# A linear-attention layer with an FP4 gate on one NeuronCore: gate and up in parts of 384 and 320 channels, two groups of tensors moved by 128 bytes

## The reference, cut to what matters

```python
q, k, v = (xn @ W + b for W, b in (Wq, bq), (Wk, bk), (Wv, bv))    # 16 heads of 64
Q, K = elu(q) + 1, elu(k) + 1
KV = einsum('bshd,bshm->bhdm', K, v)
Z = 1 / (einsum('bshd,bhd->bsh', Q, K.sum(axis=1)) + 1e-6)
o = einsum('bshd,bhdm,bsh->bshm', Q, KV, Z)
x = layer_norm(xn + o @ Wo + bo)
s = layer_norm(x + gelu(x @ W1 + b1) @ W2 + b2)
# the other branch; fq quantizes blocks of 16 along the last axis to FP4 and back
gate, up = fq(xn) @ fq(w_gate).T, fq(xn) @ fq(w_up).T              # 704 channels each
h = silu(gate) * up
g = silu(fq(h) @ fq(w_down).T)
out = src + s * g
```

## Time and profile before

| | |
|---|---|
| median of 3 runs | 1651.9 us (1649.95 to 1652.05) |
| the profiled execution, its own time | 1650.24 us |
| its span, first to last instruction | 1648.5 us |
| mean granted TensorE clock | 0.997 of full |
| TensorE (PE) busy | 1608.9 us, 98% |
| weight loads (PEld) busy | 1444.7 us, 88% |
| VectorE (DVE) busy | 1278.5 us, 78% |
| ScalarE (ACT) busy | 979.4 us, 59% |
| GpSimd (POOL) busy | 782.8 us, 47% |
| DMA, mean | 75 GB/s |

### The profile page before, as it was taken

The page is one execution under the profiler, slowest core; times in us unless marked ns, Lnnn a source line. Parts: engine busy times, 40 slices in busy tenths (PEclk is TensorE's granted clock), DMA queues, the critical chain, the costliest instruction groups (busy, mean ns, idle before and its releaser), DMA issues.

```text
span 1648.5 us, 30638 instructions
## 1 busy us (share of the span) xinstructions
PE 1608.9 (98%) x10977; PEld 1444.7 (88%) x10977; DVE 1278.5 (78%) x2485; ACT 979.4 (59%) x1770; POOL 782.8 (47%) x750
## 2 busy tenths in 40 slices
PE   7999999999999999999999999999999999999997
PEld 6878888888789998999899999989899989999897
DVE  6686664554788797888888887878788888878797
ACT  6665666655564747465665647474656656574743
POOL 4564544434242635444444536354445444363636
PEclk9999999999999999999999999999999999999999
DMA  7322323331501111122121112111121321111110
GB/s 227 126 92 85 103 77 106 103 106 58 186 15 53 52 53 52 53 109 91 47 68 53 52 53 106 53 52 53 52 63 59 103 85 58 53 52 53 52 53 26
DMA packets 92515, 123.46 MB, mean 75 GB/s; under 512 B 13503, under 2 KB 60747, under 8 KB 91342
## 3 DMA queue, kind: packets, MB, share of 16 engines
q1 hardware_dynamic: 92366, 121.51, 22.8%
HBM read 86.86 MB, written 34.62 MB: 74 GB/s over the span
## 4 chain that ended last, share of the span: by engine, by line
PE 82%; DMA 5%; DVE 5%; SPq 3%; issue 2%; ACT 1%; POOL 1%; POOLq 0%; DVEq 0%; ACTq 0%
PE QH L81 11%; PE QH L83 11%; PE QH L82 11%; PE AC L81 7%; PE AC L83 7%; PE AC L82 7%; PE GU L81 5%; PE GU L83 5%; PE GU L82 5%; DMA zb<-z_scratch 3%; PE TT L827 2%; PE DN L82 2%; PE DN L81 2%; PE DN L83 2%; SPq L404 2%
## 5 line engine op out<-in xcount | busy, mean ns | idle before, releaser
L2305 POOL TENSOR_TENSOR hb<-hb,rs_h 128x704 f32<-128x704 f32 x64 | 89.1, 1392 | 208.7 <-DVE rs_h L1676 208.7
L1244 ACT ACTIVATE hb<-GU 128x352 f32<-128x352 f32 x128 | 59.2, 462 | 216.2 <-PE GU L83 216.2
L1197 ACT ACTIVATE rh<-QH 128x512 fp32r<-128x512 f32 x256 | 151.1, 597 | 58.2 <-DVE QH L1824 53.8
L81 PE MATMUL GU<-wgh,xqh 128*128 128x352 f32 x512 | 169.8, 332 | 3.3 <-DVE hb L1669 3.3
L2311 POOL TENSOR_TENSOR hb<-hb,sn_h 128x64 f32<-128x64 f32 x64 | 18.8, 293 | 320.3 <-DVE hb L1681 320.3
L83 PE MATMUL GU<-wgh,xql 128*128 128x352 f32 x512 | 165.0, 322 | 0.0
L82 PE MATMUL GU<-wgl,xqh 128*128 128x352 f32 x512 | 165.0, 322 | 0.0
L1839 DVE TENSOR_TENSOR rl<-QH,rh 128x512 fp32r<-128x512 f32 x128 | 86.0, 682 | 85.0 <-ACT rh L1197 83.0
L81 PE MATMUL AC<-Mh,rh 128*128 128x256 f32 x512 | 145.9, 285 | 0.9 <-ACT rh L1197 0.8
L81 PE MATMUL AC<-w2h,rh 128*128 128x256 f32 x512 | 145.5, 284 | 0.0
L83 PE MATMUL AC<-Mh,rl 128*128 128x256 f32 x512 | 143.0, 279 | 0.0
(11 more groups left out here) (234 smaller groups left out, 5586.3 us busy)
## 6 DMA issues: line engine op xcount, KB each, us to landing
zb<-z_scratch SPq DMA_DIRECT2D x256, 128.0 KB, 3.0
xa<-in_L_attn_src SPq DMA_DIRECT2D x16, 512.0 KB, 4.1
xt_scratch<-xth SPq DMA_DIRECT2D x32, 256.0 KB, 2.6
xt_scratch<-xtl SPq DMA_DIRECT2D x32, 256.0 KB, 3.0
xb<-in_L_attn_src SPq DMA_DIRECT2D x16, 512.0 KB, 4.1
xnTh<-xt_scratch SPq DMA_DIRECT2D x32, 256.0 KB, 4.8
xnTl<-xt_scratch SPq DMA_DIRECT2D x32, 256.0 KB, 5.5
out<-x SPq DMA_DIRECT2D x15, 512.0 KB, 6.6
```

What stands on the lines that cost most here:

```text
L81: e.matmul(outp, lh, rh, start=start, stop=False, skip_group_check=check)
L1197: e.activation(RH[j % 4][:], src, ACT.Copy).then_inc(S[sem], 1)
L1244: e.activation(HB[i % 3][:, hf * HALF:(hf + 1) * HALF], gu_bank(i, hf)[:, 0:HALF], ACT.Tanh, scale=0.5).then_inc(S["th"], 1)
L2305: e.tensor_tensor(hb, hb, spread(rs_h[i % 2][:], 44), ALU.mult).then_inc(S["hin"], 1)
```

## The change: what it does, and the diff

`HALF` is replaced by `PARTS`: half 0 is now channels 0 to 383, half 1 channels 384 to 703. `gate_up(i, 0)` has 12 matmuls of 384 columns, `gate_up(i, 1)` 12 of 320; tanh and the two products of VectorE follow (384 and 320 columns). The order of all steps stays. `gate_up_rows`, which tells where the rows of w_gate and w_up are loaded for quantizing, follows too.

A padding of 32 columns (128 bytes) is put ahead of `xqh`, and `main_rest` is shorter by as much. What lies between moves by 128 bytes: `xqh`, `xql`, `Q32`, `eg` and `hb` from 160 to 32 modulo 256, `ksB`, `Mh`, `Ml` and the second `xb` from 96 to 224, the fourth `zb` from 160 to 32. The parts of `gate_up` now begin in `wgh` at 224, all four of them.

```diff
-HALF = 352
+PARTS = ((0, 384), (384, 704))
...
-            s, r = at // HALF, at % HALF
-            n = min(t * 128 + 128 - at, HALF - r)
-            row = (s // 2) * HALF + r
+            hf = 0 if at < 2 * PARTS[0][1] else 1
+            size = PARTS[hf][1] - PARTS[hf][0]
+            up, r = (at - 2 * PARTS[hf][0]) // size, (at - 2 * PARTS[hf][0]) % size
+            n = min(t * 128 + 128 - at, size - r)
+            row = PARTS[hf][0] + r
...
         HC = sb("hc", [128, 704])
+        sb("before_xq", [128, 32])
         xqh, xql = sb("xqh", [128, 2, D], F32R), sb("xql", [128, 2, D], F32R)
...
-        sb("main_rest", [128, 154])
+        sb("main_rest", [128, 122])
...
+                size = PARTS[hf][1] - PARTS[hf][0]
                 for part in range(2):
-                    c = hf * 704 + part * HALF
+                    c = 2 * PARTS[hf][0] + part * size
                     for kt in range(2):
-                        last = mm3(e, bank[:, part * 512:part * 512 + HALF], xqh[:, kt, o:o + 128], xql[:, kt, o:o + 128],
-                                   wgh[:, kt, c:c + HALF], wgl[:, kt, c:c + HALF], kt == 0, kt == 1)
+                        last = mm3(e, bank[:, part * 512:part * 512 + size], xqh[:, kt, o:o + 128], xql[:, kt, o:o + 128],
+                                   wgh[:, kt, c:c + size], wgl[:, kt, c:c + size], kt == 0, kt == 1)
...
-                e.activation(HB[i % 3][:, hf * HALF:(hf + 1) * HALF], gu_bank(i, hf)[:, 0:HALF], ACT.Tanh, scale=0.5).then_inc(S["th"], 1)
+                e.activation(HB[i % 3][:, PARTS[hf][0]:PARTS[hf][1]], gu_bank(i, hf)[:, 0:PARTS[hf][1] - PARTS[hf][0]], ACT.Tanh, scale=0.5).then_inc(S["th"], 1)
...
-                bank, hb = gu_bank(i, hf), HB[i % 3][:, hf * HALF:(hf + 1) * HALF]
+                size = PARTS[hf][1] - PARTS[hf][0]
+                bank, hb = gu_bank(i, hf), HB[i % 3][:, PARTS[hf][0]:PARTS[hf][1]]
...
-                e.scalar_tensor_tensor(hb, hb, 1.0, bank[:, 0:HALF], ALU.add, ALU.mult).then_inc(S["hu"], 1)
+                e.scalar_tensor_tensor(hb, hb, 1.0, bank[:, 0:size], ALU.add, ALU.mult).then_inc(S["hu"], 1)
...
-                e.tensor_tensor(hb, hb, bank[:, 512:512 + HALF], ALU.mult).then_inc(S["hh"], 1)
+                e.tensor_tensor(hb, hb, bank[:, 512:512 + size], ALU.mult).then_inc(S["hh"], 1)
```

More of the change, by code:

```diff
@@ L96, in gate_up_rows @@
         while at < t * 128 + 128:
-            s, r = at // HALF, at % HALF
-            n = min(t * 128 + 128 - at, HALF - r)
-            row = (s // 2) * HALF + r
+            hf = 0 if at < 2 * PARTS[0][1] else 1
[3 more added lines that the diff above has]
+            row = PARTS[hf][0] + r
             last = rows[-1] if rows else None
-            if n == 128 and last and last[3] == 128 and last[4] == s % 2 and last[5] + 128 * last[1] == row:
+            if n == 128 and last and last[3] == 128 and last[4] == up and last[5] + 128 * last[1] == row:
                 rows[-1] = (last[0], last[1] + 1) + last[2:]
             else:
-                rows.append((t, 1, at % 128, n, s % 2, row))
+                rows.append((t, 1, at % 128, n, up, row))
             at += n
```

## The result

| | before | after |
|---|---|---|
| median of 22 runs each | 1651.74 us | 1654.65 us |
| ratio of the runs, 95% interval | | 1.0022 (1.0015 to 1.0028) |
| the profiled execution's span | 1648.5 us | 1651.8 us |

The change makes the kernel slower by 0.22%, 3.6 us. I had forecast 4.2 us faster.

What follows compares the result with a forecast made beforehand. TensorE was taken as the bound, outside one wait a group. Half of the matmul gains, -5.6 us, plus 1.4 us for longer tanh and products gave -4.2: 1651.9 to 1647.7 us, range 1642 to 1656.

Steps and rivals of the forecast that it cites:

- Part 3, the chain: Tanh and two VectorE products of `gate_up(a, 0)`, 384 columns, take 95 ns a group more: 1.4 us lost, bounds 0 to 1.4.
- part 1: Gate and up matmuls of 384 plus 320 columns for 2 x 352: at most 4.8 us gained, at worst 2.8 lost.
- What bounds the kernel: TensorE at full clock; all its work counts except that hidden under one wait a group, 9.4 us in 13 groups.
- Part 2, the map: Map products at 224 instead of 96 go from 117.7 to 113.3 ns: at most 6.3 us gained, at worst 0.4 lost.
- rival B: Nothing turns cheap; a matmul costs a fixed part plus a part per column: 1.4 us lost, 1653.3 us, chance 0.25.
- Rival C: New sizes and places fall into a dearer way, 324.9 ns a gate_up pair: +4.6 us, 1656.5 us, chance 0.17.
- C's sign: `gate_up(., 0)` matmuls of 384 columns at 176 ns or more would show the dearer, slower case.
- Part 3, the other tiles: Longer tanh and products outside `gate_up(a, 0)` lie beside matmuls, as 2.8 us against some 1.5 in tile c: no cost.
- Part 4: Everything else, such as three loads fewer in the first stage and moved tensors, costs nothing.
- the prediction's last sign of being wrong: w2, `down` or `h_proj`, unchanged in size and place, shifting by more than the map and `gate_up` together.

Runs made afterwards that it cites:

- map_two: The kernel before, with one of at_step's three map products (rows' high part by map's low part) left out: ratio 1.0001 (0.9992 to 1.0010).
- TensorE alone: Nothing of the layer computed, only matmul blocks after transposes at varied places and sizes; 320, 352, 384 columns at (32, 224) cost 146.4, 160.0, 173.2 ns.
- parts_only: Parts of 384 and 320 columns at the old places, without the 128-byte shift, against the kernel before: ratio 1.0029 (1.0019 to 1.0040).

## Why the prediction was wrong, by its own steps

*Part 3, the chain: the term that holds the loss.* The 95 ns (27 + 34 + 34) for tanh and products were right to the nanosecond. What failed is that the block ahead of them was put at nothing: `gate_up(a, 0)` itself takes 0.205 us longer, and the chain is 0.299 us longer, not 0.095. The chain that I read showed the block, one step ahead of the tanh:

```profile
1035.71 0.17 PE GU L83
1035.88 0.02 issue
```

I counted the block's 384 columns in part 1, paid back by the 320 of `gate_up(a, 1)`. They aren't paid back there. `den_sums` waits for `q_elu` anyway, so the block's length is free on TensorE (2.26 us to `den_sums` at all three sizes), but the denominators wait for its products. `gate_up(a, 1)` gives 0.16 us back on TensorE; `gate_up(a, 0)` takes 0.205 + 0.095 on the chain. The term's upper bound of 1.4 us should have been 0.299 x 14, about 4.

*What bounds the kernel.* "Everything else of TensorE is on it" failed as well. I took the earlier trace rows, where TensorE hardly waits, for a proof that TensorE is the bound outside the one wait. map_two refutes it for the 19 us from the transposes to `turn_x1`, a quarter of each group: 60 us of matmuls less gave 1.0001.

*Part 2, the map.* That it turns cheap at 224 was right. The gain of up to 6.3 us was mis-placed: it lies in the stretch where TensorE is not the bound, and all map products together gave 0.5 us from start to start.

*Part 1, gate and up.* The step from "352 is five and a half times 64 columns" to a good price for 384 and 320 was a reading of two sizes, 256 and 512, stretched to sizes that no row had. In TensorE alone 384 + 320 costs 173.3 + 146.6 = 319.9 ns, 2 x 352 costs 320.0. The additive rule of rival B holds there for these three sizes, with 13.3 ns a matmul where the Trainium skill ("TensorE: Matmul & The Clock Gate", Back-to-back issue gap) has 2.5 for a single matmul by itself. In the changed kernel the pair costs 321.6: on 576 pairs 1.0 us lost, not 4.8 gained. Rival C's 324.9 isn't reached, but its kind of loss is there in part: `gate_up(a, 0)` is at 176.7 in all of groups 1 to 13, the value that the prediction gave as C's sign. A pair with such a block costs 323.4.

*Part 3, the other tiles.* "For the other tiles the longer halves lie beside matmuls" was wrong for tile c: the products of its half 0 end 0.078 us behind GpSimd's result on VectorE's way to the norm.

*Part 4* held as far as the traces show it: `den_sums` of group 0 starts at 431.4 us before and at 431.6 after. Of TensorE's blocks whose sizes and places didn't change none takes more than some 0.05 us a group longer (`f_step` behind `den_sums`, 4.20 us before and 4.26 after), so the prediction's last sign of being wrong isn't what was seen.

*Range and chances.* That the measured 1.0022 lies within the range of 1642 to 1656 is luck: the range was made of part 1's and part 2's prices, and the loss came from the chain. It falls between B (+1.4) and C (+4.6). The chance of 0.49 for faster stood on two gains of which one rested on an untested reading, and both on TensorE as the bound.

What stays open: of the 3.6 us, 1.7 are accounted for by the three lines together; whether the rest is in the transfers of the denominators or in the first and last groups isn't settled. Nor is it known why some places and entries give the cheap state, or why 384 columns cost 173.3 ns in some blocks and 176.7 in others.

## What to carry to other kernels

An engine that never waits is not yet the bound: two engines can keep step so closely that both look full, and the test is to leave out some of one's work (here a third of one step's matmuls) and look at the time. When sizes in a row are made unequal, look for the block ahead of a fixed wait: on its own engine its length may be free, but what hangs on its end starts later by all of it. And for a round trip through DRAM ask what stands ahead of it in its engine's queue: two lines of order were worth 0.56% here, more than anything in parts or places.

## What the hardware showed that I had not expected

- Two equal streams of fp32r matmuls of 256 columns, at the same clock, cost 113.3 or 117.7 ns each, for tens of matmuls on end, and TensorE alone shows it: it is no contention with other engines. With moving minus stationary start at -64 modulo 256 bytes the cheap state is possible; the other places gave 116.7 to 120.0. In the cheap kind of place a block can still stay at 117.7, by what ran before it.
- With 320, 352 and 384 columns TensorE alone had no state like the 113.3, at the eight places tried: 146.6, 160.0, 173.3, that is 0.4167 ns a column and 13.3 ns. Single pairs of places were dearer (161.1, 176.7), and in the changed kernel 24 of 62 blocks of 384 are at 176.7, in `parts_only` none.
- With 60 us of matmuls left out, on an engine that is busy for 98% of the span, the time stayed within 0.1% (1.0001, 0.9992 to 1.0010).
